# Issuing the output-row moves from SP instead of ACT in a DeltaNet and mixture-of-experts kernel

## The chip, the cores and the metric

One core of a Trainium2 chip runs the whole program. The metric is the device time in microseconds (us) of one execution; the median of three runs is quoted. One further execution is recorded by the hardware profiler. The engines are PE (TensorE, matrix products), ACT (ScalarE), DVE (VectorE), POOL (GpSimd) and SP (SyncE, which here only waits and issues DMAs). Each engine takes its own instructions strictly in order. ACT and SP both can issue DMAs; each has a queue of its own, q10 and q1 in the profile.

## The reference

The input is x of shape (2, 2048, 256). The first layer is a gated delta rule with 8 heads of 128 and three Householder steps per token, the second a mixture of 8 experts of which each token uses 2. Cut to what matters here:

```python
q = _short_conv(x @ Wq, conv_q)            # 4 taps over time, then silu
k = _short_conv(x @ Wk, conv_k)            # 3 keys per token
v = _short_conv(x @ Wv, conv_v)            # 3 values per token
def step(S, inp):                          # one token, state S is 128 x 128 per head
    S = S * jnp.exp(gt)[..., None, None]
    for i in range(nh):
        kS = jnp.einsum('bhd,bhde->bhe', ki, S)
        S = S + bi[..., None, None] * (ki[..., None] * (vi - kS)[:, :, None, :])
    o = jnp.einsum('bhd,bhde->bhe', qt, S)
o = o * jax.lax.rsqrt(jnp.mean(o * o, -1, keepdims=True) + 1e-05) * rms_weight
o = o * jax.nn.silu(x @ Wg)
x = _layernorm(x + o @ Wo)
x = _layernorm(x + experts(x))             # top 2 of 8, F = 816
```

## The kernel before

A setup stage splits x and the weights into pairs of 16-bit parts and stores them to HBM. Then comes the main loop, from about 100 to 4000 us, and last the router and the experts. The change touches only the main loop.

**Blocks.** The work of the loop is cut in 128 blocks: 16 (batch, head) pairs, each with 8 stretches of 256 tokens. The order is all 16 pairs of a stretch `tb`, then the next stretch. A block of 256 tokens has 8 chunks `c` (or `u`) of 32 tokens. For each chunk the three delta steps and the query make a 128-row triangular system, which is inverted in levels (`level_x`, `level_t`, `level_tt` on PE, copied out by `mask_x` on DVE and `keep_t`, `keep_tt` on ACT). Then the chunks run one after another through the state: `from_state`, `solve`, `update` on PE, with `keep_w(c)` on ACT writing the solution to `w_sol`. Rows 96 to 127 of `w_sol` hold the outputs of the 32 tokens.

**Bodies.** The engines are software pipelined. One body, written out by hand for each engine as a fixed list, works on five blocks at once: `k0` is the newest, `k1` to `k4` the ones one to four bodies older. Semaphores (class `Count`) connect the lists. For block `k3` the body of ACT ends the chunks with `keep_w(7, k3)`, then moves the output rows, and some operations later squares them:

- `move_outputs(k3)` (L1015 to L1021) waits for `keep_w(7)` and for the free buffer (`scaled`), and issues four DMAs, each of 32 partitions by two chunks, from `w_sol` to `o_rows` (64 rows of 512 B). This changes the partitions on which the rows lie, from 32 to all 128.
- `square_outputs(k3)` (L1024 to L1029) waits until all four have landed (`moved`), then computes the sums of squares.

After `square_outputs` ACT has `keep_t(6, 0)` and `keep_tt(6, 0)`, for which PE waits in `residual(0)` (L785, matmuls L792 and L793). Before `residual(0)` PE has `project(4)` (L692). Two operations behind `move_outputs` ACT has `keep_tt(4, 0)` (L1002), for which PE waits in `level_t(5, 0)` (L768, L780).

**SP.** For each (tb, head), that is for each body, SP does in this order:

- `body`: the small table `t_cur`;
- `load_next`: it waits until the last projection and the last convolution tap (`tapped`) of the block before are done, and loads the inputs of the next block: `x_cur` (L577, 259 KB), `w_cur` (L580, 1024 KB), `c_cur` (L581), `g_cur` (L582);
- `outputs`: it clears 128 rows of the experts' input (L600, 256 KB), waits for `y_buf` of the block five bodies back and stores it (L606, 128 KB);
- `pieces`: for the heads 0 to 13 it loads a piece of the experts' weights (L629, 224 KB, heads 0 to 11) and stores one that POOL has split (L639, 224 KB, heads 2 to 13), behind a wait for POOL's `e_low` (L1367).

`w_cur` and `x_cur` have two buffers each, so a load issued at the start of a body is needed about one body later.

Of the kernel before, what the change touches and what calls it, by code (L numbers as in the profile page):

```python
# [32 lines left out]
B, T, D = 2, 2048, 256  # L33
KT = D // P
H, NH, DH = 8, 3, 128
TAPS = 4
CH = 32
UN = 8
TB = CH * UN
NTB = T // TB  # L40
NIT = B * H * NTB
# [78 lines left out]
def at_least(eng, sem, value):  # L120

    if isinstance(value, int) and value <= 0:
        return
    eng.wait_ge(sem, value)


def build(nc, x_t, x_rows, w_all, w_z, conv_w, a_log, dt_bias, rms_w, w_o, consts, masks,
# [8 lines left out]
    with ctx:  # L136
# [244 lines left out]
        with ExitStack() as loop_scope:  # L381
            scope = loop_scope

            def ring(name, size, shape, dt):
# [52 lines left out]
            moved = [sem("moved0"), sem("moved1")]  # L437
            e_in = [sem("piece_in0"), sem("piece_in1")]
            e_out = [sem("piece_out0"), sem("piece_out1")]
            (sp_waited, act_waited, cleared, x_waited, pool_waited, e_high, e_low, zeroed) = map(sem, (  # L440
                "sp_waited", "act_waited", "cleared", "x_waited", "pool_waited", "piece_high", "piece_low", "zeroed"))
            squared, q_squared, g_made, scaled = map(sem, ("squared", "q_squared", "g_made", "scaled"))
            gate_done, ln_made, norm_made, o_squared, var_ln_made, rstd_made = map(sem, (
                "gate_done", "ln_made", "norm_made", "o_squared", "var_ln_made", "rstd_made"))
# [126 lines left out]
            with nc.Block() as block:  # L571
                @block.sync
                def _(sp):
                    def load(tb, head, res):

                        b, h = head // H, head % H
                        sp.dma_start(x_cur[res][:, :, :, 0:PW].rearrange("p a b c -> p (a b) c"),  # L577
                                     x_dram.rearrange("p (a c) -> p a c", a=2 * KT)[:, :, bass.ds(b * XW + tb * TB, PW)])\
                            .then_inc(loaded[res], 16)
                        sp.dma_start(w_cur[res][:].rearrange("p a b c -> p (a b c)"), w_dram[h]).then_inc(loaded[res], 16)  # L580
                        sp.dma_start(c_cur[res][:], conv_sb[:, h]).then_inc(loaded[res], 16)  # L581
                        sp.dma_start(g_cur[res][:], g_parts[:].rearrange("p n a -> p (n a)")[:, bass.ds((head * NTB + tb) * UN, UN)])\  # L582
                            .then_inc(loaded[res], 16)

                    clear_rows = x_slots.rearrange("(a b) d -> a (b d)", b=2)

                    def body(tb, head, new=True):

                        n = B * H * tb + head
                        if new:  # L590
                            done(sp, stated, 7, n - 8)
                            sp.sem_inc(sp_waited, 1)
                            sp.dma_start(t_cur[head % 8][:].rearrange("p a b -> p (a b)"),
                                         tables[:].rearrange("p n a b -> p (n a b)")[:, bass.ds((head * NTB + tb) * (4 * UN), 4 * UN)])\
                                .then_inc(tabled[head % 4], 16)

                    def outputs(tb, head, new=True):
                        n = B * H * tb + head
                        if new:
                            sp.dma_start(clear_rows[bass.ds(n * P, P), :], no_rows[:]).then_inc(cleared, 16)  # L600
                        d = n - STORED
                        if not isinstance(n, int) or 0 <= d < NIT:
                            done(sp, rows_kept, "outputs", d)
                            sp.sem_inc(sp_waited, 1)
                            dst = y_dram[d] if isinstance(d, int) else y_dram.rearrange("n p t -> (n p) t")[bass.ds(d * P, P), :]
                            sp.dma_start(dst, y_buf[(head - STORED) % 2][:]).then_inc(stored[(head - STORED) % 2], 16)  # L606

                    def load_next(tb, head):
                        n = B * H * tb + head
                        done(sp, projected, 7, n - 1)  # L610
                        sp.sem_inc(sp_waited, 1)
                        done(sp, tapped, 6, n - 1)
                        sp.sem_inc(sp_waited, 1)
                        at_least(sp, g_made, n)
                        sp.sem_inc(sp_waited, 1)
                        if head + 1 < B * H:
                            load(tb, head + 1, (head + 1) % 2)
                        else:
                            load(tb + 1, 0, 0)

                    def load_piece(e, c):

                        buf, (k, q) = e_raw[c % 2], (c // 4, c % 4)
                        at_least(sp, e_low, 12 * e + c - 1)
                        sp.sem_inc(sp_waited, 1)
                        src = (up_w, gp_w, down_w)[k].rearrange("e p c -> (e p) c")
                        c0, cut = q * QUARTER, (FT - 1) * D
                        if c < 11:
                            sp.dma_start(buf[:], src[bass.ds(e * P, P), c0:c0 + QUARTER]).then_inc(e_in[c % 2], 16)  # L629
                            return  # L630
                        sp.dma_start(buf[:, 0:cut - c0], src[bass.ds(e * P, P), c0:cut]).then_inc(e_in[1], 16)
                        sp.dma_start(buf[0:64, cut - c0:], src[bass.ds(e * P, 64), cut:]).then_inc(e_in[1], 16)
                        sp.dma_start(buf[64:65, cut - c0:], down_b[bass.ds(e, 1), :]).then_inc(e_in[1], 16)
                        sp.dma_start(buf[65:P, cut - c0:], src[bass.ds(e * P + 65, P - 65), cut:]).then_inc(e_in[1], 16)

                    def store_piece(e, c):
                        sp.wait_ge(e_low, 12 * e + c + 1)
                        sp.sem_inc(sp_waited, 1)
                        sp.dma_start(e_dram[c // 4][bass.ds(e * P, P), :, (c % 4) * QUARTER:(c % 4 + 1) * QUARTER],  # L639
                                     e_pair[c % 2][:]).then_inc(e_out[c % 2], 16)  # L640

                    def pieces(e, head):

                        if head < 12:
                            load_piece(e, head)
                        if 2 <= head <= 13:
                            store_piece(e, head - 2)

                    load(0, 0, 0)
                    for head in range(B * H):  # L650
                        body(0, head)
                        load_next(0, head)
                        outputs(0, head)
                        pieces(0, head)
                    with sp.Fori(1, NTB - 1) as tb:
                        for head in range(B * H):
                            body(tb, head)
                            load_next(tb, head)
                            outputs(tb, head)
                            pieces(tb, head)  # L660
                    for head in range(B * H):
                        body((NTB - 1), head)
                        if head + 1 < B * H:
                            load_next((NTB - 1), head)
                        outputs((NTB - 1), head)
                        pieces((NTB - 1), head)
                    for i in range(max(STORED, 4)):
                        outputs(NTB, i, new=False)
                    for i in range(2):
                        sp.wait_ge(e_out[i], 16 * (NPIECE // 2))  # L670
                        sp.wait_ge(stored[i], 16 * (NIT // 2))
                    sp.wait_ge(cleared, 16 * NIT)
# [260 lines left out]
                def _(act):  # L933
# [78 lines left out]
                        a(w_sol[k.i % 2][:, c], chain(k), ACT.Copy).then_inc(sol_kept.sem, 1)  # L1012

                    @at_stage
                    def move_outputs(k):  # L1015

                        done(act, sol_kept, 7, k.n)
                        at_least(act, scaled, k.n - 1)
                        act.sem_inc(act_waited, 1)
                        for c in range(4):  # L1020
                            act.dma_start(o_rows[k.i % 2][c * CH:(c + 1) * CH], w_sol[k.i % 2][96:128, c::4, :]).then_inc(moved[k.i % 2], 16)  # L1021

                    @at_stage
                    def square_outputs(k):  # L1024
                        act.wait_ge(moved[k.i % 2], 64 * (k.turn(2) + 1))
                        done(act, rows_kept, "queries", k.n - 1)
                        for i in range(2):
                            last = a(o_sq[:, i], o_rows[k.i % 2][:, i], ACT.Square, accum_out=o_sum[:, i:i + 1])
                        last.then_inc(o_squared, 1)  # L1029
# [12 lines left out]
                    def body(k0, k1, k2, k3, k4):  # L1042
# [12 lines left out]
                        keep_w(7, k3)  # L1055
                        silu(1, k0)
                        keep_t(4, 0, k1)
                        move_outputs(k3)
                        keep_tt(4, 0, k1)
                        first_tap(3, k0)  # L1060
                        keep_t(3, 1, k1)
# [986 lines left out]
```

## Time and profile before

| | |
|---|---|
| median of three runs | 4994.92 us (4980.66 to 4997.5) |
| profiled execution | 4980.66 us, its span 4978.8 us |
| busy in the span | PE 4230.5 us (85%), DVE 3658.3 (73%), ACT 3285.0 (66%), POOL 1648.1 (33%) |
| mean granted TensorE clock | 0.927 of 2.4 GHz |
| DMA, whole span | 490.64 MB, mean 99 GB/s |

The span reaches from the first to the last instruction. Busy time leaves out waiting and the issuing of DMAs. A row of the timeline says when an instruction started, how long it took, on which engine and line it is, what it writes and reads, and in brackets how long the engine had been idle before it and what ended that idle time. "issue" there means that the engine waited for nothing that the profile shows but its own sequencer. A "q" behind an engine's name is its sequencer, which issues DMAs. A DMA's row shows the issuing alone; the landing of the data is a separate number. 1.00 in a clock column is 2.4 GHz, 0.50 is 1.2 GHz.

### The profile page before, as it was taken

How to read it: one execution, taken by the hardware profiler on the slowest of the kernel's cores; microseconds unless marked ns; L12 is line 12 of the kernel's file. 1: busy time of each engine (PE TensorE's matmuls, PEld its weight loads, DVE VectorE, ACT ScalarE, POOL GpSimd, SP SyncE). 2: the span in 40 equal slices, each digit the busy share in tenths (PEclk: the TensorE clock that was granted, in tenths of full speed). 3: DMA queues.
4: the chain of work that ended last, by engine and by line, in shares of the span. 5: the costliest groups of instructions: out<-in, count | busy, mean ns of one | idle time of the engine just before them, and what ended most of it. 6: DMA issues, size and time to landing. Idle time of an engine off the chain costs nothing. (4 is left out here: it accounts for less than half of the span.)

```text
span 4978.8 us, 148669 instructions
## 1 busy us (share of the span) xinstructions
PE 4230.5 (85%) x47876; PEld 3759.0 (75%) x47876; DVE 3658.3 (73%) x10194; ACT 3285.0 (66%) x9028; POOL 1648.1 (33%) x1615
## 2 busy tenths in 40 slices
PE   2889988989898888898888898889889867599992
PEld 1788878888887777788788787888878745488882
DVE  6888888888888778788888788888888722344446
ACT  3777777777777677777777777777777611255552
POOL 3434333334433333343334343333434202200004
PEclk6999999999999999999999999999999877699996
DMA  6232223222223333222222222322222133366664
GB/s 234 69 95 73 66 77 86 79 70 77 77 71 70 76 77 70 70 77 79 82 75 77 77 67 77 92 76 67 75 77 75 43 88 108 123 236 227 230 236 140
DMA packets 363269, 490.64 MB, mean 99 GB/s; under 512 B 94080, under 2 KB 308096, under 8 KB 343680
## 3 DMA queue, kind: packets, MB, share of 16 engines
q1 hardware_dynamic: 304784, 437.06, 29.8%
q10 hardware_dynamic: 51568, 27.04, 1.9%
q0 software_dynamic: 6144, 16.79, 1.1%
q8 instruction: 419, 6.86, 0.6%
q14 instruction: 354, 2.90, 0.2%
HBM read 352.02 MB, written 107.75 MB: 92 GB/s over the span
## 5 line engine op out<-in xcount | busy, mean ns | idle before, releaser
L1134 DVE SCALAR_TENSOR_TENSOR conv_acc<-bank,c_cur,conv_acc 128x256 f32<-128x256 f32 x2688 | 1265.9, 477 | 274.3 <-ACT conv_acc L944 261.2
L692 PE MATMUL bank<-x_cur,w_cur 128*128 128x259 f16 (+1 forms) x6144 | 913.2, 288 | 29.4 <-DVE v_rows L1122 26.3
L1329 POOL TENSOR_TENSOR squares<-kq_t 128x768 f32<-128x768 f32 x128 | 187.7, 1467 | 1909.4 <-ACT kq_t L955 1909.4
L1195 DVE CAST_PREDICATED xs_lev<-mask,bank 128x256 f16<-128x256 uint16 x1536 | 662.2, 431 | 198.1 <-PE bank L756 174.4
L1002 ACT ACTIVATE invt<-bank 128x256 f16<-128x256 f32 x1280 | 509.7, 398 | 400.3 <-issue 374.5
L993 ACT ACTIVATE inv<-bank 128x256 f16<-128x256 f32 x1536 | 607.0, 395 | 167.8 <-PE bank L768 158.1
L692 PEld LDWEIGHTS bank<-x_cur,w_cur 128*128 128x128 f16 (+1 forms) x6144 | 577.7, 102 | 124.7 <-DVE v_rows L1122 27.2
L780 PE MATMUL bank<-invt,xs_lev 128*128 128x64 f16 x5120 | 379.9, 199 | 309.4 <-ACT invt L1002 305.2
L780 PEld LDWEIGHTS bank<-invt,xs_lev 128*128 128x128 f16 x5120 | 293.2, 101 | 341.5 <-ACT invt L1002 254.2
L944 ACT ACTIVATE conv_acc<-bank,c_cur 128x256 f32<-128x256 f32 x896 | 425.3, 475 | 156.5 <-PE bank L692 149.4
L824 PE MATMUL bank<-w_sol,k_rows 128*128 128x128 f32 x2048 | 474.6, 315 | 4.5 <-ACT w_sol L1012 4.1
L756 PE MATMUL bank<-inv,n_high 128*128 128x64 f16 x6144 | 450.8, 197 | 13.0 <-issue 2.7
L819 PE MATMUL bank<-rhs,inv_t 128*128 128x128 f32 x2048 | 447.4, 306 | 2.0 <-DVE rhs L1209 1.6
L813 PE MATMUL bank<-state,kq_t 128*128 128x128 f32 x2048 | 434.6, 304 | 8.5 <-DVE state L1216 7.7
L1342 POOL TENSOR_TENSOR n_t<-n_t,cst 128x512 f32<-128x512 f32 x256 | 326.1, 1274 | 329.5 <-DVE n_t L1162 329.5
L768 PE MATMUL bank<-xs_lev,invt 128*128 128x64 f16 x5120 | 377.1, 198 | 23.5 <-DVE xs_lev L1195 11.2
L756 PEld LDWEIGHTS bank<-inv,n_high 128*128 128x128 f16 x6144 | 321.2, 101 | 97.2 <-issue 43.5
L1209 DVE SCALAR_TENSOR_TENSOR rhs<-bank,t_cur,v_rows 128x128 f32<-128x128 f32 x1024 | 345.0, 337 | 30.8 <-PE bank L813 30.6
L1012 ACT ACTIVATE w_sol<-bank 128x128 f32<-128x128 f32 x1024 | 284.1, 278 | 118.4 <-PE bank L819 118.4
L1216 DVE SCALAR_TENSOR_TENSOR state<-state,t_cur,bank 128x128 f32<-128x128 f32 x1024 | 347.1, 339 | 11.5 <-PE bank L824 11.3
L1320 POOL TENSOR_TENSOR decay<-decay_tok,cst 128x512 f32<-128x512 f32 x256 | 320.7, 1274 | 99.5 <-ACT decay_tok L967 81.6
L768 PEld LDWEIGHTS bank<-xs_lev,invt 128*128 128x128 f16 x5120 | 292.4, 103 | 64.6 <-issue 26.7
(241 smaller groups left out, 10672.6 us busy)
## 6 DMA issues: line engine op xcount, KB each, us to landing
w_cur<-w_parts_scratch SPq DMA_DIRECT2D x128, 1024.0 KB, 7.1
ew<-e_parts_scratch SPq DMA_DIRECT2D x117, 896.0 KB, 6.2
x_cur<-x_parts_scratch SPq DMA_DIRECT2D x128, 259.0 KB, 7.0
x_slots<-no_rows SPq DMA_DIRECT2D x128, 256.0 KB, 7.1
e_parts_scratch<-e_pair SPq DMA_DIRECT2D x96, 224.0 KB, 6.0
o_rows<-w_sol ACTq DMA_DIRECT2D x512, 32.0 KB, 4.6
y_scratch<-y_buf SPq DMA_DIRECT2D x128, 128.0 KB, 6.3
y_in<-y_scratch SPq DMA_DIRECT2D x32, 512.0 KB, 4.1
```

What stands on the lines that cost most here:

```text
L692: last = mm(bank[i % 2][:, 0:PW], w_cur[k.i % 2][:, wp, kt, c * P:(c + 1) * P].bitcast(BF16 if wp else F16), x_cur[k.i % 2][:, xp, kt, 0:P ...
L756: last = mm(packed(LEVX[:, u * HP:(u + 1) * HP], l), n_high[k.i % 2][g][:, u], half(inv[k.i % R_LEV][g][:, u], l, 0), start=True, stop=True)
L768: last = mm(packed(LEVT[:, u * HP:(u + 1) * HP], l), by[:, u], half(xs_lev[g][l - 1][:, u], l, 0), start=True, stop=True)
L780: last = mm(packed(LEVTT[:, u * HP:(u + 1) * HP], l), xs_lev[g][l - 1][:, u], half(invt[k.i % R_LEV][g][:, u], l, 1), start=True, stop=True)
L813: mm(chain(k), kq_t[k.i % R_KQ][:, c].rearrange("p a b -> p (a b)"), state[:, k.i % (B * H)], start=True, stop=True).then_inc(ks_made.sem, 1)
L819: mm(chain(k), inv_t[k.i % R_INV][:, c], rhs[k.i % 2][:], start=True, stop=True).then_inc(sol_made.sem, 1)
L824: mm(chain(k), k_rows[k.i % R_ROWS][:, c], w_sol[k.i % 2][:, c], start=True, stop=True).then_inc(upd_made.sem, 1)
L944: a(conv_acc[(k.n + i) % 2][:], bank[i % 2][:, 0:TB], ACT.Copy, scale=c_cur[k.i % 2][:, c, 0:1])\
L993: a(half(inv[k.i % R_LEV][g][:], l, 0), packed(halves(LEVT), l), ACT.Copy).then_inc(t_kept.sem, 1)
L1002: a(half(dst, l, 1), packed(halves(LEVTT), l), ACT.Copy).then_inc(tt_kept.sem, 1)
L1134: v.scalar_tensor_tensor(acc, bank[at % 2][:, i:i + TB], c_cur[k.i % 2][:, c, i:i + 1], acc, ALU.mult, ALU.add).then_inc(tap_step.sem if i ...
L1195: v.copy_predicated(half(xs_lev[g][l - 1][:], l, 0), half(mask4[:, l], l, 0).bitcast(U16), packed(halves(LEVX), l)).then_inc(x_kept.sem, 1)
```

## The change

The four moves of a block are issued by SP and no longer by ACT. `move_outputs` is now a function of SP. It first waits that `o_rows` is free and then, ahead of each of the four DMAs, for the chunk `keep_w(4 + c)` of which the DMA takes the rows, where ACT had waited once for `keep_w(7)`. It stands at the end of SP's list, behind `load_next`, for the block three bodies older. In the same list the clear and the store of `y_buf` go from `outputs` into `body`, ahead of `load_next`, and `pieces` goes ahead of `load_next` too. After the last loads, SP's five closing turns call `body` (without the table and the clear) and `move_outputs`. ACT's list is unchanged but for the missing call.

```diff
-                    def outputs(tb, head, new=True):
-                        n = B * H * tb + head
                         if new:
                             sp.dma_start(clear_rows[bass.ds(n * P, P), :], no_rows[:]).then_inc(cleared, 16)
                         d = n - STORED
...
                             sp.dma_start(dst, y_buf[(head - STORED) % 2][:]).then_inc(stored[(head - STORED) % 2], 16)
+
+                    def move_outputs(n, i):
+
+                        if not isinstance(n, int) or 0 <= n < NIT:
+                            at_least(sp, scaled, n - 1)
+                            sp.sem_inc(sp_waited, 1)
+                            for c in range(4):
+                                done(sp, sol_kept, 4 + c, n)
+                                sp.sem_inc(sp_waited, 1)
+                                sp.dma_start(o_rows[i % 2][c * CH:(c + 1) * CH], w_sol[i % 2][96:128, c::4, :]).then_inc(moved[i % 2], 16)
...
                     with sp.Fori(1, NTB - 1) as tb:
                         for head in range(B * H):
                             body(tb, head)
+                            pieces(tb, head)
                             load_next(tb, head)
-                            outputs(tb, head)
-                            pieces(tb, head)
+                            move_outputs(B * H * tb + head - 3, head - 3)
...
                     for i in range(max(STORED, 4)):
-                        outputs(NTB, i, new=False)
+                        body(NTB, i, new=False)
+                        move_outputs(NIT + i - 3, i - 3)
...
                     @at_stage
-                    def move_outputs(k):
-
-                        done(act, sol_kept, 7, k.n)
-                        at_least(act, scaled, k.n - 1)
-                        act.sem_inc(act_waited, 1)
-                        for c in range(4):
-                            act.dma_start(o_rows[k.i % 2][c * CH:(c + 1) * CH], w_sol[k.i % 2][96:128, c::4, :]).then_inc(moved[k.i % 2], 16)
...
                         keep_t(4, 0, k1)
-                        move_outputs(k3)
                         keep_tt(4, 0, k1)
```

The order of the first and of the last stretch of 16 heads is changed in the same way as that of the loop.

## Rows read from the trace of the kernel before

**Rows 1.** Waits, whole run: who waited for whom, us in total, times, longest.
```profile
ACT invt L1002 <- issue: 374.5, 126, 4.6
PE bank L780 <- ACT invt L1002: 305.2, 126, 4.1
...
ACT o_sq L1028 <- DMA o_rows<-w_sol: 109.6, 88, 4.0
...
PE bank L792 <- ACT invt L1002: 55.2, 56, 2.9
```

**Rows 2.** Timeline of SP, one body: start us, us, what [idle before].
```profile
1130.54 0.62 SPq L577 DMA_DIRECT2D x_cur<-x_parts_scratch  x1
...
1132.49 3.30 SPq L582 DMA_DIRECT2D g_cur<-g_parts  x1
1136.01 0.53 SPq L600 DMA_DIRECT2D x_slots<-no_rows  x1
1136.91 0.34 SPq L606 DMA_DIRECT2D y_scratch<-y_buf  x1
...
1138.20 0.62 SPq L639 DMA_DIRECT2D e_parts_scratch<-e_pair  x1
...
1159.53 0.61 SPq L577 DMA_DIRECT2D x_cur<-x_parts_scratch  x1
```

**Rows 3.** Timeline of ACT, the same body.
```profile
1134.46 0.28 ACT L1012 ACTIVATE w_sol<-bank 128x128 f32<-128x128 f32 x1
...
1135.50 1.97 ACTq L1021 DMA_DIRECT2D o_rows<-w_sol  x3
1137.58 0.38 ACT L1002 ACTIVATE invt<-bank 128x256 f16<-128x256 f32 x1 [2.27 <-issue]
...
1142.62 0.31 ACT L1028 ACTIVATE o_sq<-o_rows 128x128 f32<-128x128 f32 x1 [1.58 <-DMA o_rows<-w_sol]
```

**Rows 4.** Timeline of PE, the same body.
```profile
1138.02 0.29 PE L780 MATMUL bank<-invt,xs_lev 128*128 128x64 f16 x4 [1.75 <-ACT invt L1002]
...
1141.77 0.84 PE L692 MATMUL bank<-x_cur,w_cur 128*128 128x259 f16 x6
1143.90 0.23 PE L792 MATMUL bank<-inv,n_high 128*128 128x128 f16 x1 [1.30 <-ACT invt L1002]
```

**Rows 5.** SP and ACT in two other bodies; windows view (clock third from last).
```profile
3080.53 0.62 SPq L577 DMA_DIRECT2D x_cur<-x_parts_scratch  x1
...
3091.03 0.31 ACT L1028 ACTIVATE o_sq<-o_rows 128x128 f32<-128x128 f32 x1
...
3108.11 0.61 SPq L577 DMA_DIRECT2D x_cur<-x_parts_scratch  x1
...
636.26 0.31 ACT L1028 ACTIVATE o_sq<-o_rows 128x128 f32<-128x128 f32 x1 [3.17 <-DMA o_rows<-w_sol]
...
655.95 0.62 SPq L577 DMA_DIRECT2D x_cur<-x_parts_scratch  x1
...
639.00:646.00 7.00, 7.00 (x43) 6.85 (x43) 3.92 (x14) 3.09 (x9) 4.02 (x4) 0.51 0.01 2
```

**Rows 6.** L577 (durations, first and last start), its first full body, and L1021's landings.
```profile
L577 SPq DMA_DIRECT2D x_cur<-x_parts_scratch x128: 577/602/669, 100.9 to 3889.3; - x128
...
186.56 0.58 SPq L577 DMA_DIRECT2D x_cur<-x_parts_scratch  x1
...
DMA to landing us min/median/max: 1.9/4.6/7.4
```

**Rows 7.** DMA view, 1139 to 1141 us, all queues.
```profile
DMA packets 681, 0.68 MB, mean 342 GB/s; under 512 B 209, under 2 KB 605, under 8 KB 660
```

**Rows 8.** The same, 1141 to 1143 us, by queue: packets, MB, share of 16 engines.
```profile
q1 hardware_dynamic: 310, 0.25, 36.9%
...
q10 hardware_dynamic: 40, 0.02, 2.8%
```

**Rows 9.** Timeline of POOL, the same body's piece.
```profile
1127.63 1.04 POOL L1367 TENSOR_TENSOR e_pair<-e_raw,e_pair 128x448 bf16<-128x448 f32 x1
```

More of the change, by code:

```diff
@@ L439, in build @@
             e_out = [sem("piece_out0"), sem("piece_out1")]
-            (sp_waited, act_waited, cleared, x_waited, pool_waited, e_high, e_low, zeroed) = map(sem, (
-                "sp_waited", "act_waited", "cleared", "x_waited", "pool_waited", "piece_high", "piece_low", "zeroed"))
+            (sp_waited, cleared, x_waited, pool_waited, e_high, e_low, zeroed) = map(sem, (
+                "sp_waited", "cleared", "x_waited", "pool_waited", "piece_high", "piece_low", "zeroed"))
             squared, q_squared, g_made, scaled = map(sem, ("squared", "q_squared", "g_made", "scaled"))
@@ L651, in _ @@
                         body(0, head)
+                        pieces(0, head)
                         load_next(0, head)
-                        outputs(0, head)
-                        pieces(0, head)
+                        move_outputs(B * H * 0 + head - 3, head - 3)
                     with sp.Fori(1, NTB - 1) as tb:
@@ L657, in _ @@
                             body(tb, head)
+                            pieces(tb, head)
                             load_next(tb, head)
-                            outputs(tb, head)
-                            pieces(tb, head)
+                            move_outputs(B * H * tb + head - 3, head - 3)
                     for head in range(B * H):
                         body((NTB - 1), head)
+                        pieces((NTB - 1), head)
                         if head + 1 < B * H:
                             load_next((NTB - 1), head)
-                        outputs((NTB - 1), head)
-                        pieces((NTB - 1), head)
+                        move_outputs(B * H * (NTB - 1) + head - 3, head - 3)
                     for i in range(max(STORED, 4)):
-                        outputs(NTB, i, new=False)
+                        body(NTB, i, new=False)
+                        move_outputs(NIT + i - 3, i - 3)
                     for i in range(2):
@@ L1014, in move_outputs @@
                     @at_stage
-                    def move_outputs(k):
-                        done(act, sol_kept, 7, k.n)
-                        at_least(act, scaled, k.n - 1)
-                        act.sem_inc(act_waited, 1)
-                        for c in range(4):
-                            act.dma_start(o_rows[k.i % 2][c * CH:(c + 1) * CH], w_sol[k.i % 2][96:128, c::4, :]).then_inc(moved[k.i % 2], 16)
-                    @at_stage
                     def square_outputs(k):
```

## The prediction

> **What bounds the kernel now.** I read four views in this order.
>
> First the whole run's waits [rows 1]. ACT, an engine that computes, stands idle for 374.5 us in 126 stalls "by issue" ahead of `keep_tt(4, 0)` (L1002). PE stands idle for 305.2 us in 126 stalls waiting for that same line. ACT then waits 109.6 us for the moved rows (L1028), and PE 55.2 us for what ACT does behind that wait. So the four `move_outputs` DMAs cost ACT, and through it PE, about 2.4 us in every body.
>
> That sum is not yet a gain, so second comes one body, engine by engine, with its zero at the start of SP's `x_cur` DMA, 1130.54 us [rows 2]. ACT ends the issue of the four moves at +6.93 us, and they have held it idle for 2.27 us [rows 3]. Its `square_outputs` starts at +12.08, held 1.58 us by the landing of the moves. PE idles 1.75 us at L780, finishes `project(4)` at about +12.07, idles another 1.30 us and starts `residual(0)` at +13.36 [rows 4]. The next `x_cur` is issued at +28.99 [rows 2].
>
> Third, the length of a body splits in two: D, from `x_cur` to the start of `square_outputs`, and R, from there to the next `x_cur`. Here D = 12.08 and R = 16.91. In the body at 3080.53, D = 10.50 and R = 17.08 [rows 5]. The same two rows, read for all 123 bodies from 186.56 to 3889.3 us [rows 6], give a mean D of 12.75 and a mean R of 17.36, with 89 bodies' R below 17.3. R hardly depends on D. A body lasts as long as its moved rows are late, plus a fixed rest. The mean body is (3889.3 - 186.56)/123 = 30.10 us.
>
> Fourth, what sets D. The last move is issued by +6.93 but its rows are used at +12.08, 5.15 us later, although the shortest landing in the run took 1.9 us [rows 6]. The DMA engines are full: between +8.5 and +10.5 us they move 342 GB/s [rows 7], and between +10.5 and +12.5 come the last 40 packets of ACT's queue (q10), beside 310 of SP's queue (q1) [rows 8]. The 1.28 MB of `x_cur` and `w_cur` stand in front of them.
>
> **The change, part by part.**
>
> *ACT loses the four issues.* That removes 2.27 us of idle in this body, 374.5/126 = 2.97 us on average [rows 1, 3]. PE's stall at L780 goes with it. If nothing else held, PE would reach the end of `project(4)` at 12.07 - 1.75 = +10.3 us, and ACT `square_outputs` at 12.08 - 1.58 - 2.27 = +8.2.
>
> *SP issues them instead, behind `load_next`.* SP ends `g_cur` at +5.25 [rows 2]. The neighbours of such an issue there take 0.34 to 0.62 us, and 0.22 us (no wait) to 0.37 us (a wait and an increment) lie between them. Four issues with five waits take 4 x 0.5 + 5 x 0.33 = 3.7 us, so the last ends near +8.9, against +6.93 before. `keep_w(7)` is done at +4.2 [rows 3] and holds nothing up. Queued behind the moves on SP are `t_cur`, the clear, the `y` store, the pieces and the next loads. None is due within 15 us, so that part costs nothing; if the cover were gone each would be 1 to 4 us late.
>
> *The landing, D'.* The lower bound is issue plus the shortest landing: 8.9 - 0.5 + 1.9 = +10.3. The moves are now in SP's own queue behind the loads, so they can't pass them; that queue is still at work after +10.5 [rows 8]. What helps: the clear, the `y` store, `e_raw` and `e_store` (256 + 128 + 224 + 224 KB) no longer compete with the moves from behind. What hurts: for 14 of 16 heads `e_raw` and `e_store` now go ahead of the loads. POOL ends the piece at 1128.67, 1.87 us before `x_cur` [rows 9]; two issues (0.36 + 0.62) and two waits fit in that, so `x_cur` is not issued later, but up to 448 KB lie in front of it. Upper bound: at the 342 GB/s of [rows 7], 1.3 us later than now, 12.75 + 1.3 = 14.0. I take 12.4, near today's 12.75, because it is backlog and not issue that sets it.
>
> The Trainium skill ("DMA: Bandwidth & Descriptors", section "Queues, rings and completion order") says that each DMA engine takes packets from its queues in turn, so that moves on ACT's queue would overtake part of the loads and lose that on SP's. The trace does not bear out much overtaking, since 40 q10 packets start more than 3 us after the last issue ended [rows 3, 8]; by the rule the sum would go by the upper bound, 14.0.
>
> *The rest, R'.* Its work is untouched. But the idle of PE is now in one piece: it ends `project(4)` at +10.3 and starts `residual(0)` 1.28 us after `square_outputs` (13.36 - 12.08), at 12.4 + 1.3 = +13.7. That is 3.4 us of idle in place of 1.75 and 1.30 apart. Of 46 bodies whose L780 stall [rows 4] is 2.7 us or more, 39 have TensorE's granted clock at its lower level (1.2 GHz) shortly after; of 75 with a shorter one, 38. Until now that low stretch fell mostly before `residual(0)`, in time that the moves cost anyway. It would now fall in R, where PE is nearly always busy. Price: after 3.17 us of waiting at 636.26 the clock is 0.51 for 7 us and R is 19.69, 2.8 more than 16.91, 0.4 us for each us at the low level [rows 5]. A usual low stretch lasts half as long: 1.4 us, times 39/46, 1.2 us. A part is in the mean of 17.36 already, so I add 1.1. Bounds: 0 and 2.8.
>
> *The edits to the order* (clear and `y` store in `body`, pieces ahead of `load_next`) have no price beyond D'. The five bodies after the last load have no loads in front of the moves: a gain of about 5 us at most in all.
>
> **Sum.** D' + R' = 12.4 + 17.36 + 1.1 = 30.86 us, 0.76 more than 30.10, times 123 = +93 us. The profiled execution took 4980.66 us (span 4978.8), the lowest of the three runs; the median is 4994.92. From the one 5074 comes out, from the other 5088. I say 5080 us.
>
> **Rivals.**
>
> *A: relief arrives.* If the moves land by about +9.5, ACT and PE are held no longer. The body falls to PE's own work: in the body at 3080.53 PE had no other wait and took 27.58 us [rows 5], and 1.75 of it is the stall of [rows 4], so some 26. That is -3.5 to -4 us, 123 times: 4500 to 4600 us. For it: 305.2 us of PE's waits point at the issue alone [rows 1]. Against it: the landing follows the load backlog, and SP issues later, not earlier. It decides on D' below 10.5. Chance 0.17.
>
> *B: the stall moves, the clock does not fall into R, or D' is near the lower bound.* With D' of 11.5 to 12.7 and R' of 17.36 a body takes 28.9 to 30.1 us: 4830 to 4990 us. For it: some bodies passed 2.9 us stalls at full clock. Against: 39 of 46. It ends on the other side or at no change. Chance 0.23.
>
> *C: the whole queue slips* behind the pieces. D' = 13.7 and R' = 18.5 give 32.2, +2.1 us, 5235 us. For it: the 448 KB. Against: they are issued 1.9 us before the loads, when the engines are idle. Chance 0.15. The page's rule named above would end here too.
>
> *The change does nothing*, since SP reaches the moves only when they are late: this is the forecast's own mechanism, and it would show as no change if the clock held. It is in B.
>
> **How the numbers follow.** Forecast 0.45 (its own range 4990 to 5170), A 0.17, B 0.23, C 0.15. The range leaves out A and the ends of B and C: 4860 to 5240. Within 0.3% (15 us) is what a measurement of this kernel can't tell from no change. Faster: A and two thirds of B, 0.32. Same: the rest of B and a little of the forecast, 0.10. Slower: 0.58.
>
> **What would show it.** "ACT invt L1002 <- issue" gone. The wait of ACT at L1028 up from 109.6 to some 450 us (3.5 us in each body), with D' about 12.4. PE's waits for L1002 at L780 nearly gone, those at L792 up from 55 to some 400 us. A low clock within 5 us after `residual(0)` in most bodies and R above 18. The prediction is wrong if `square_outputs` starts before +10.5 us (A), or if R stays at 17 (B).

## The result, and the profile after

The changed kernel takes 5211.15 us (median of four executions, 5154.57 to 5220.62) against 4988.82 us (four, 4980.66 to 4997.5; the 4994.92 us quoted for the kernel before are the median of three of these). The measured ratio, which is not that of the two medians, is 1.0422, with a 95% interval of 1.0344 to 1.0500: slower by 4.2%. The medians lie 222 us apart. The forecast was 5080 us, slower by 1.7%. The sign and the chain of waits came out as forecast, and the time lies in the wide range (4860 to 5240) but outside the 4990 to 5170 that belonged to the forecast itself. The size came out at more than twice what was forecast.

The profiled execution of the changed kernel took 5212.94 us, its span 5211.1 us. The mean granted clock of TensorE fell from 0.927 to 0.883. PE is busy for 4387.1 us in place of 4230.5, though it computes the same.

The waits of the whole run, changed kernel (engine line waited for: us, times, longest):

```profile
ACT o_sq L1027 <- DMA o_rows<-w_sol: 447.7, 119, 7.6
DVE v_sum L1223 <- issue: 374.4, 118, 6.9
PE bank L800 <- ACT invt L1010: 361.5, 111, 7.2
...
ACT invt L1010 <- PE bank L788: 48.9, 134, 4.5
```

The first two rows of [rows 1] are gone: no stall "by issue" ahead of `keep_tt(4, 0)` (now L1010) and next to none of PE in `level_t`. In their place ACT's wait for the moved rows has gone from 109.6 to 447.7 us, and PE's wait in `residual(0)` (now L800) from 55.2 to 361.5. Together ACT waits about as long as before (374.5 + 109.6 = 484 against 448). The stall has moved.

The `x_cur` loads, and the landings of the moves, changed kernel (durations in ns; first and last start in us):

```profile
L577 SPq DMA_DIRECT2D x_cur<-x_parts_scratch x128: 582/639/714, 101.4 to 4125.3; - x128
...
L613 SPq DMA_DIRECT2D o_rows<-w_sol x512: 585/638/1616, 189.9 to 4223.0; - x171
...
DMA to landing us min/median/max: 1.8/3.7/6.3
```

The first full body starts at 185.98 us, so the mean body is (4125.3 - 185.98)/123 = 32.03 us, 1.93 more than 30.10. Times 123 that is 237 us, about the whole difference of the spans (5211.1 - 4978.8 = 232). The change costs nothing outside the main loop.

One body of the changed kernel, SP, then ACT, then PE (timeline; start, us, what, idle before):

```profile
1507.58 0.65 SPq L577 DMA_DIRECT2D x_cur<-x_parts_scratch  x1
...
1509.62 2.96 SPq L582 DMA_DIRECT2D g_cur<-g_parts  x1
1512.85 3.11 SPq L613 DMA_DIRECT2D o_rows<-w_sol  x4
...
1541.58 0.65 SPq L577 DMA_DIRECT2D x_cur<-x_parts_scratch  x1
...
1519.64 0.31 ACT L1027 ACTIVATE o_sq<-o_rows 128x128 f32<-128x128 f32 x1 [3.62 <-DMA o_rows<-w_sol]
...
1516.84 0.84 PE L700 MATMUL bank<-x_cur,w_cur 128*128 128x259 f16 x6
1520.93 0.29 PE L800 MATMUL bank<-inv,n_high 128*128 128x128 f16 x1 [3.25 <-ACT invt L1010]
```

SP ends the fourth move 8.38 us after `x_cur`; `square_outputs` starts at +12.06 (D), held 3.62 us. PE is through with `project(4)` at about +10.1 and stands 3.25 us ahead of `residual(0)`. All of that is as forecast. But from `square_outputs` to the next `x_cur` it takes 21.94 us (R). The windows view of that stretch shows why (PE busy and instructions, PEld, DVE, ACT, POOL, then the granted clock):

```profile
1521.00:1524.50 3.50, 3.50 (x26) 3.22 (x27) 2.08 (x6) 3.21 (x8) 2.58 (x2) 0.50 0.02 5
1524.50:1528.00 3.50, 3.50 (x22) 3.50 (x21) 1.64 (x5) 0.97 (x5) 2.48 (x2) 0.50 0.00 0
1528.00:1531.50 3.50, 3.50 (x22) 3.33 (x22) 1.98 (x9) 0.69 (x4) 0.56 (x1) 0.50 0.00 0
1531.50:1535.00 3.50, 3.50 (x30) 3.06 (x28) 2.17 (x8) 2.15 (x6) 0.71 (x1) 0.80 0.00 0
1535.00:1538.50 3.50, 3.50 (x46) 3.24 (x44) 3.41 (x12) 3.49 (x10) 2.62 (x3) 1.00 0.00 0
```

For over 10 us after the idle the clock stays at 1.2 GHz (0.50), and PE, busy throughout, gets 22 to 26 matmuls done in 3.5 us in place of 46. DVE is busy for 1.6 to 2.1 and ACT for 0.7 to 3.2 of each 3.5 us.

The same numbers for all 123 bodies, read from the timeline and the clock's records:

| mean per body, us | before | changed |
|---|---|---|
| body | 30.10 | 32.03 |
| D | 12.75 | 12.35 |
| of it, the last move's issue ends at | 7.80 | 8.34 |
| of it, the last move lands at | 12.57 | 12.28 |
| R | 17.36 | 19.68 |
| low clock, whole body | 2.80 | 7.10 |
| low clock in R, from 1.3 us behind the start of `square_outputs` (about where `residual(0)` starts) | 0.40 | 5.79 |
| bodies with none in R | 108 of 123 | 20 of 123 |

The 20 bodies of the changed kernel with no low clock in R have a mean R of 17.25 us, as before. In 35 bodies it is low for some 3.3 us and R is 18.72. In 50 it is low for more than 6.9 us, on average 10.5, and R is 21.52. That is 0.41 us for each us at the low level, (21.52 - 17.25)/10.5, the price that the prediction took from one body.

### The profile page after: what moved, and what is told of

Read it like the earlier page. It is cut to its first block and busy times, and to the rows that moved or that the text cites. A ratio compares the mean times of both kernels' runs of the same rounds, so it can differ in the third digit from the quotient of the medians.

```text
span 5211.1 us, 149412 instructions
## 1 busy us (share of the span) xinstructions
PE 4387.1 (84%) x47876; PEld 3922.9 (75%) x47876; DVE 3641.6 (70%) x10194; ACT 3283.0 (63%) x9028; POOL 1648.1 (32%) x1615
## 5 line engine op out<-in xcount | busy, mean ns | idle before, releaser
L700 PE MATMUL bank<-x_cur,w_cur 128*128 128x259 f16 (+1 forms) x6144 | 884.0, 281 | 39.9 <-DVE v_rows L1120 26.3
L700 PEld LDWEIGHTS bank<-x_cur,w_cur 128*128 128x128 f16 (+1 forms) x6144 | 564.7, 100 | 131.7 <-DVE v_rows L1120 27.2
L1010 ACT ACTIVATE invt<-bank 128x256 f16<-128x256 f32 x1280 | 511.2, 399 | 50.1 <-PE bank L788 48.9
L832 PE MATMUL bank<-w_sol,k_rows 128*128 128x128 f32 x2048 | 494.8, 326 | 3.0 <-ACT w_sol L1020 2.7
L800 PE MATMUL bank<-inv,n_high 128*128 128x128 f16 x1024 | 173.9, 249 | 361.5 <-ACT invt L1010 361.5
L827 PE MATMUL bank<-rhs,inv_t 128*128 128x128 f32 x2048 | 469.1, 318 | 2.5 <-DVE rhs L1207 1.8
L821 PE MATMUL bank<-state,kq_t 128*128 128x128 f32 x2048 | 461.9, 321 | 8.7 <-DVE state L1214 7.7
L800 PEld LDWEIGHTS bank<-inv,n_high 128*128 128x128 f16 x1024 | 112.6, 112 | 394.0 <-ACT invt L1010 300.4
L764 PEld LDWEIGHTS bank<-inv,n_high 128*128 128x128 f16 x6144 | 306.5, 98 | 120.5 <-issue 74.2
L788 PE MATMUL bank<-invt,xs_lev 128*128 128x64 f16 x5120 | 368.0, 194 | 27.1 <-issue 27.0
L1027 ACT ACTIVATE o_sq<-o_rows 128x128 f32<-128x128 f32 x256 | 76.9, 301 | 447.7 <-DMA o_rows<-w_sol 447.7
```

Source lines behind the costliest of these rows:

```text
L700: last = mm(bank[i % 2][:, 0:PW], w_cur[k.i % 2][:, wp, kt, c * P:(c + 1) * P].bitcast(BF16 if wp else F16), x_cur[k.i % 2][:, xp, kt, 0:P ...
L764: last = mm(packed(LEVX[:, u * HP:(u + 1) * HP], l), n_high[k.i % 2][g][:, u], half(inv[k.i % R_LEV][g][:, u], l, 0), start=True, stop=True)
L788: last = mm(packed(LEVTT[:, u * HP:(u + 1) * HP], l), xs_lev[g][l - 1][:, u], half(invt[k.i % R_LEV][g][:, u], l, 1), start=True, stop=True)
L821: mm(chain(k), kq_t[k.i % R_KQ][:, c].rearrange("p a b -> p (a b)"), state[:, k.i % (B * H)], start=True, stop=True).then_inc(ks_made.sem, 1)
L827: mm(chain(k), inv_t[k.i % R_INV][:, c], rhs[k.i % 2][:], start=True, stop=True).then_inc(sol_made.sem, 1)
L832: mm(chain(k), k_rows[k.i % R_ROWS][:, c], w_sol[k.i % 2][:, c], start=True, stop=True).then_inc(upd_made.sem, 1)
```

## The experiments

Times are medians; ratios are to the kernel before, run on the same chip. "Body", D and R are means of 123 bodies of the profiled execution, and the low clock in R is counted as in the table above.

### e3, e4: the two halves of the change

The change moves the issue and reorders SP's list. e3 does the first alone (the moves on SP behind `load_next`, and behind them `outputs` and `pieces` as before), e4 the second alone (ACT keeps the moves):

```diff
# e3, against the changed kernel
                         body(tb, head)
-                        pieces(tb, head)
                         load_next(tb, head)
                         move_outputs(B * H * tb + head - 3, head - 3)
+                        outputs(tb, head)
+                        pieces(tb, head)
```

```diff
# e4, against the changed kernel
                         load_next(tb, head)
-                        move_outputs(B * H * tb + head - 3, head - 3)
...
                         keep_t(4, 0, k1)
+                        move_outputs(k3)
                         keep_tt(4, 0, k1)
```

> The moves are issued by SP directly behind load_next as in the changed kernel, but the clear, the store of y and the pieces stay behind them, in the order of the kernel before. Theory L: the order part matters little, 5150 to 5260 us, D 12.3 to 13. Rival C of the prediction (the pieces in front of the loads make the whole queue slip): this undoes it, D falls to about 11.5 and the time to 5000 to 5080. Rival S (SP's order): most of the loss gone.

> The order of SP's list as in the changed kernel (clear, store and pieces ahead of load_next), but ACT issues the moves as in the kernel before. Theory L: within 1% of the kernel before, a little faster if anything (the clear no longer competes with the moves), 4930 to 5000 us; the 374.5 us of issue stalls on ACT stay, D 12.3 to 12.8. Rival C: slower by 2% or more, since the pieces delay the loads and with them the moves.

e3: 5157.04 us, ratio 1.0327 (1.0295 to 1.0360); body 31.55, D 12.26, R 19.29, 5.4 us of low clock in R. e4: 4982.25 us, ratio 0.9978 (0.9951 to 1.0005); body 30.03, D 12.55, R 17.47. Its waits are those of the kernel before (last row: the moved rows, `square_outputs`):

```profile
ACT invt L996 <- issue: 364.4, 126, 5.0
...
PE bank L774 <- ACT invt L996: 294.1, 126, 4.5
...
ACT o_sq L1022 <- DMA o_rows<-w_sol: 111.0, 89, 4.0
```

So the issue by SP behind the loads makes most of the loss. The reordering alone is no change, as the prediction had it; with the moves on SP the median goes from 5157 to 5211 us with it, but the two intervals still touch, so that this part is left open.

The landing is nearly independent of who issues. In e4 the last issue ends at +7.61 and the rows land at +12.39. In the changed kernel, three quarters of a us later on another queue, they land at +12.28. The Trainium skill ("DMA: Bandwidth & Descriptors", section "Issuing engines are not separate DMA queues") says that DMAs run on the same 16 DMA engines whichever engine starts them. These two landings agree with it, 0.11 us apart.

What the moves stand behind is not the bulk of the loads alone. In the mean of the changed kernel's bodies `w_cur` (1024 KB) has landed at +8.10 us, `c_cur` (14 KB) at +9.36, `g_cur` (2 KB) at +11.54 and the last move at +12.28. In the body shown above, SP's queue keeps the DMA engines only 45.6% busy from 8.4 to 10.4 us after `x_cur` (1516 to 1518, DMA view):

```profile
DMA packets 455, 0.27 MB, mean 133 GB/s; under 512 B 292, under 2 KB 434, under 8 KB 434
```

In the kernel before it was 342 GB/s in nearly the same stretch of a body [rows 7]. So in these 2 us it is not full DMA engines that hold the moves of the changed kernel, and yet they land at about the same time. How much of D is due to the two small loads is not shown: no run leaves them out alone.

### e1: the moves ahead of the loads

```diff
                         pieces(tb, head)
-                        load_next(tb, head)
                         move_outputs(B * H * tb + head - 3, head - 3)
+                        load_next(tb, head)
```

> The changed kernel, with the four moves ahead of load_next in SP's list and not behind it. Nothing else differs. Theory L (the moves land late because the 1.28 MB of loads stand in front of them, and what they lose comes back as one idle stretch of PE in which the clock falls): the moves then wait for keep_w(7) alone, some 4 us into the body, and land 2 to 3 us after the last issue, that is about when ACT arrives. The wait of ACT at square_outputs falls from 447.7 us to below 100, PE's at residual(0) from 361.5 to below 60, the clock stays up, and a body takes 26 to 28 us in place of 32.0: 4400 to 4650 us, well below both kernels. Rival S (SP is too slow an issuer, or its new list is at fault): SP's list has the same instructions, so the time stays near 5200. Rival Q (on SP's queue the moves lose the turn that they had on ACT's): they still share the queue with the clear and the store, and only a part comes back: 4950 to 5100.

4466.65 us, ratio 0.8944 (0.8914 to 0.8974), granted clock 0.954. It is the fastest kernel of all, 10.6% below the one before and 14% below the changed one. Its first full body starts at 192.49 us; its `x_cur` loads and the landings of its moves:

```profile
L577 SPq DMA_DIRECT2D x_cur<-x_parts_scratch x128: 583/642/1591, 101.7 to 3403.4; - x128
...
L613 SPq DMA_DIRECT2D o_rows<-w_sol x512: 585/633/1917, 186.9 to 3490.2; - x171
...
  ACT o_sq L1027: 3.9, 2
...
DMA to landing us min/median/max: 1.8/2.0/6.2
```

The body is (3403.4 - 192.49)/123 = 26.11 us. The median landing falls from 3.7 to 2.0 us, ACT's wait for the rows from 447.7 to 3.9 us in the whole run (third row), and PE's idle from 3.59 to 0.27 us in each body. The moves are the same four DMAs by the same engine; only what stands in front of them differs. One body, SP:

```profile
1403.26 5.12 SPq L613 DMA_DIRECT2D o_rows<-w_sol  x4
1408.88 0.66 SPq L577 DMA_DIRECT2D x_cur<-x_parts_scratch  x1
```

The loads still come once per body, and no wait of the main loop for `x_cur` or `w_cur` shows in the list.

The gain over the changed kernel has two parts. PE's idle is 3.32 us per body shorter, and the clock is low for 0.42 us of a body in place of 7.10, which at 0.41 us for each is worth 2.7 us. Together that is 6.1 us, against 5.92 (32.03 - 26.11) measured.

### e7: how much of that is ACT's issuing

The kernel before, ACT still issuing, but the loads held back until the rows of the block in flight are squared:

```diff
                         n = B * H * tb + head
+                        at_least(sp, o_squared, n - 2)
+                        sp.sem_inc(sp_waited, 1)
```

> The kernel before, the moves still issued by ACT, but load_next waits also until square_outputs of the block whose rows are being moved has been made, so that no load stands ahead of the moves or beside them. Against the version with the moves on SP ahead of the loads (4467 us, 26.1 us per body) this prices the issuing by ACT alone. If ACT's four issues cost PE what the chain of waits says (305 to 375 us in all, 2.5 to 3 us in each body), the body takes 28.5 to 29 us and the kernel 4760 to 4830 us, and the wait at square_outputs is nearly gone. If the issues cost nothing once the landing is early (PE catches up behind them), it is about 4470 to 4550 us. If instead the later loads come too late for the next body, it is above 4993 us, with PE or ACT waiting for x_cur or w_cur.

4755.21 us, ratio 0.9559 (0.9518 to 0.9600); body 28.30, both just below what was expected if the issues cost what the waits say. The wait for the moved rows is down to 7.9 us in the whole run, and the issue remains:

```profile
ACT invt L1004 <- issue: 305.7, 126, 3.5
PE bank L782 <- ACT invt L1004: 238.1, 126, 3.1
```

So, from before (30.10) by way of e7 (28.30) to e1 (26.11), the loads in front of the moves cost 1.80 us per body and ACT's issuing 2.19. e7 and e1 also differ in the order of SP's list, which e4 showed to be worth nothing in the kernel before, and in when the loads start. But PE's idle per body, 2.05 us in e7 and 0.27 in e1, accounts for most of the 2.19. The issuing is what the change set out from in [rows 1]: it is real, 269 us in 123 bodies, but the changed kernel, which took it away first, got nothing for it.

### e6: half the weights

The changed kernel, with the low parts of `w_cur` loaded once at the start and never again, 512 of 1024 KB per body (every head is computed with the low parts of head 0, so e6 does not compute the same).

```diff
-                        sp.dma_start(w_cur[res][:].rearrange("p a b c -> p (a b c)"), w_dram[h]).then_inc(loaded[res], 16)
+                        sp.dma_start(w_cur[res][:, 0].rearrange("p b c -> p (b c)"), w_dram[h][:, 0:KT * HC]).then_inc(loaded[res], 16)
```

> The changed kernel, but w_cur is reloaded in each body with its high parts alone, 512 KB in place of 1024; the low parts are those of head 0 throughout, so the reload of the low parts is left out. Theory (the moves lie behind the backlog of the loads in SP's queue): 512 KB less at some 340 GB/s land 1.5 us earlier, D falls from 12.35 to about 10.9, the wait at square_outputs from 3.6 to about 2.1 us, R from 19.7 to about 18.5 as less of it runs at the low clock: 29.4 us per body, 4850 to 4950 us. Rival (SP's own issuing, the last of which ends at 8.3 us, and the moves' own time of flight set D): D stays within 0.3 us of 12.35 and the time within 1% of 5211.

4633.4 us, ratio 0.9325 (0.9290 to 0.9360); body 27.55, D 9.75, R 17.80, ACT's wait for the rows 154.3 us in the run. The last move is issued at +7.67 and lands at +9.61. The direction is that of the backlog, and the rival (SP's issuing sets D) falls. The size was missed, in D (2.6 us less, not 1.5) and in the time (4633 us, not 4850 to 4950). The 2.6 us are not all transfer time of 512 KB: `w_cur` itself landed 1.97 us earlier (6.13 against 8.10), which is 266 GB/s and not the 340 that I had divided by. `g_cur` behind it landed 3.16 us earlier (8.38 against 11.54), and SP was through with issuing the moves 0.67 us earlier. From its last issue to the landing e6 takes 1.94 us, near the 1.8 of the shortest landing, so there SP's issuing does set D. With D below 10.5 the kernel is where the prediction had put its case A; the body of some 26 us of that case is not reached (27.55).

### e2, e8, e5: filling PE's idle

If the long idle is what sends the clock down, useless work on PE in that idle must make the changed kernel faster. The first matmul of `project(4)` is repeated (22 times in e2 and e5, 10 in e8; some 2.4 and 1.1 us of PE), into the bank that the real one then overwrites:

```diff
+                        for _ in range(22 if c == 4 else 0):
+                            mm(bank[i % 2][:, 0:PW], w_cur[k.i % 2][:, 0, 0, c * P:(c + 1) * P].bitcast(F16),
+                               x_cur[k.i % 2][:, 0, 0, 0:PW].bitcast(F16), start=True, stop=True)
```

e2 and e8 are the changed kernel with them, e5 is the kernel before with them.

> The changed kernel, with the first matmul of project(4) repeated 22 times ahead of the real ones, 259 columns each, 2.4 us of PE work at the high clock inside the 3.6 us that PE idles before residual(0). The output is the same. Theory L, by its clock part: the moves land at the same time (D 12.4), but the clock no longer falls, so R goes from 19.7 back to about 17.1 and a body takes 29.5 us: 4880 to 4950 us, although more work is done. If the clock is not what makes R longer (rival: ACT and DVE, which have slipped behind PE, need the time), R stays at 19.7 and the time stays at 5200 or rises by what of the added work does not fit.

> The changed kernel with the first matmul of project(4) repeated 10 times (about 1.1 us of PE work in each body, in the idle ahead of residual(0)), between the changed kernel with none (5211 us, 5.8 us of low clock in R) and with 22 (5029 us, 1.3 us of it). If the clock in R is what costs, by how long PE has idled before it, the time lies between the two, 5080 to 5150 us, and the mean R of those bodies that have no low clock in it stays at 17.3 whatever the count. Rival: the time lost in R comes with the late rows themselves: then R with no low clock in it would already be above 18.

> The kernel before, with the first matmul of project(4) repeated 22 times (the same repeats that took the changed kernel from 5211 to 5029 us). They compute nothing that is used. In the kernel before PE idles only about 0.45 us (PE's waits for the line behind residual(0), 55.2 us over 123 bodies) to 1.3 us ahead of residual(0), and 108 of its 123 bodies have no low clock in R. If the repeats help only by keeping TensorE from the one long idle stretch, they must cost here: 2.4 us of PE work less the idle that they fill, +1.0 to +1.9 us in each body, 5110 to 5230 us. Rival: the repeats help whatever the issue of the moves (by an order or a timing that they shift): then this one is faster too, below 4950 us.

| | us | ratio (interval) | body | D | R | low clock in R | PE's wait in residual(0), whole run |
|---|---|---|---|---|---|---|---|
| changed | 5211.15 | 1.0422 (1.0344 to 1.0500) | 32.03 | 12.35 | 19.68 | 5.79 | 361.5 |
| e8, 10 repeats | 5083.35 | 1.0237 (1.0186 to 1.0287) | 31.23 | 12.48 | 18.75 | 3.18 | 201.8 |
| e2, 22 repeats | 5029.35 | 1.0072 (1.0051 to 1.0093) | 30.69 | 12.49 | 18.20 | 1.26 | 106.6 |
| e5, before with 22 | 5172.86 | 1.0419 (1.0376 to 1.0462) | 31.78 | 12.79 | 18.99 | 0.28 | |

More work makes the changed kernel 3.5% faster (5029 against 5211 us), with D and ACT's wait where they were (463.5 us in e2). The rows are still late in e2:

```profile
ACT o_sq L1030 <- DMA o_rows<-w_sol: 463.5, 121, 8.0
...
PE bank L803 <- ACT invt L1013: 106.6, 78, 4.4
```

The same repeats make the kernel before 4.2% slower, where they have no long idle to fill. That rules out that they help by themselves. e8 lies between, inside the expected 5080 to 5150. R of the bodies without low clock is 17.06 in e8 and 17.4 in e2, so late rows alone, without a low clock behind them, do not lengthen R. e2 did not come back all the way, and its 5029 us miss the expected 4880 to 4950: 94 of its bodies run R at full clock, but the other 29 do not, and their mean R is 20.9. Where the idle would have been short the repeats themselves should take time, as they do in e5; in e2 this part was not measured by itself.

### e9: the idle in one piece without SP

Is it SP's new list, or only the place of the idle? e9 is the kernel before, with ACT's call moved down:

```diff
                         keep_t(4, 0, k1)
-                        move_outputs(k3)
                         keep_tt(4, 0, k1)
...
+                        move_outputs(k3)
                         square_outputs(k3)
```

> The kernel before (ACT issues, SP's order as it was), with ACT's move_outputs called directly ahead of square_outputs in place of ahead of keep_tt(4, 0). So PE's stall at level_t(5, 0) is gone and all of its idle comes in one piece ahead of residual(0), as in the changed kernel, though SP's list is untouched. Theory (a low stretch that begins at residual(0) lasts about twice as long as one that begins at level_t: with 2.7 to 3.3 us of idle ahead 7.5 us against 4.0): R rises to 19.5 or more with 6 us or more of low clock in it, D to about 13.5 to 14 as the issue ends near +11 us; 33 to 34.5 us per body, 5340 to 5520 us. Rival (the long low stretches come from SP's new list or from the moves on its queue): R stays at 17.4 to 18.5 with low stretches of 3.4 us as in the kernel before, 31 to 32.5 us per body, below 5290 us.

5501.1 us, ratio 1.1063 (1.1017 to 1.1110); body 34.17, D 13.99, R 20.18, 7.6 us of low clock in R, all as the theory had it. In one body PE idles 3.09 us and the clock then is at the low level for some 10 us (timeline, then windows):

```profile
512.30 0.22 PE L792 MATMUL bank<-inv,n_high 128*128 128x128 f16 x1 [3.09 <-ACT invt L1002]
```

```profile
513.00:516.50 3.50, 3.50 (x26) 3.24 (x23) 2.42 (x5) 2.69 (x6) 2.81 (x3) 0.50 0.02 5
516.50:520.00 3.50, 3.50 (x19) 3.50 (x20) 1.09 (x6) 0.69 (x3) 1.77 (x2) 0.50 0.00 0
520.00:523.50 3.50, 3.50 (x24) 3.04 (x23) 2.20 (x7) 0.92 (x4) 1.27 (x1) 0.55 0.00 0
523.50:527.00 3.50, 3.50 (x42) 3.40 (x41) 2.88 (x10) 3.37 (x7) 0.58 (x1) 1.00 0.00 0
```

Over all bodies: in the kernel before 46 idles of 2.7 us or more end at `level_t(5, 0)`. A low stretch goes with 39 of them; 35 of these last 3.4 us and one 10.2. At `residual(0)` the changed kernel has 72 such idles, each with a low stretch, of which 45 last 10.2 or 13.7 us; e9 has 108, of which 68 are followed by 10.2 us or more.

But these idles are also longer, 4.1 us in the mean in the changed kernel and 4.5 in e9 against 3.1 at `level_t`. Among idles between 2.7 and 3.5 us alone, 1 of 42 at `level_t` goes with 10 us or more, against 13 of 26 (changed) and 12 of 23 (e9) at `residual(0)`. So the place counts at equal length too. The length counts beside it: in the 38 bodies of the changed kernel and the 79 of e9 in which the clock had fallen more than 1 us before PE started again, no low stretch was shorter than 6.8 us, and at `level_t` in the kernel before it never fell that early. That e9 is slower than the changed kernel goes with its longer idles and its later landing (D 13.99), not with the place alone.

### e10: squaring later

The changed kernel, with `square_outputs(k3)` four operations later on ACT, so that `residual(0)` no longer stands behind the late rows, and DVE's `sum_squares(k3)` (L1223) three operations later, ahead of `keep_v(0, k1)`:

```diff
-                        square_outputs(k3)
                         keep_t(6, 0, k1)
                         keep_tt(6, 0, k1)
                         silu(3, k0)
                         keep_w(4, k2)
+                        square_outputs(k3)
```

> The changed kernel with square_outputs four operations later in ACT's list (behind keep_t(6, 0), keep_tt(6, 0), silu(3) and keep_w(4)) and DVE's sum_squares of it three later, ahead of keep_v(0). The moved rows land as late as before, but PE's residual(0) no longer waits behind them. Theory (the lateness costs only through what is queued behind the wait on ACT): PE's idle of 3.6 us in each body goes, no low clock in R, 27.5 to 29 us per body, 4650 to 4850 us; what is left of ACT's wait is 1 to 2.5 us in each body. Rival: the wait only moves; PE and DVE then wait for keep_w(4), first_tap(4) or v_sum, and the time stays above 5050 us.

5140.88 us, ratio 1.0308 (1.0259 to 1.0358), body 31.67, so the rival was right. ACT's wait for the rows falls to 264.0 us, but PE now stands a few operations further on:

```profile
PE bank L739 <- DVE v_sum L1223: 280.1, 116, 6.2
ACT o_sq L1027 <- DMA o_rows<-w_sol: 264.0, 109, 5.9
```

PE needs there what DVE does behind `sum_squares`. PE still idles 2.97 us per body, and 6.3 us of R are at the low clock. The late rows are squared on ACT, their sums are needed on DVE and the rows again on POOL, and to defer the first two by a few operations was not enough.

## Why the prediction came out as it did

*What bounds the kernel* held in its first half: D is the landing of the moved rows behind the loads; e1, e4, e6 and e7 show it from four sides. Not shown is that full DMA engines make it late: in the changed kernel these move 133 GB/s from +8.4 to +10.4 in place of 342, and D' is nearly the same. That R is a "fixed rest" did not hold.

*ACT loses the issues, PE's first stall goes*: right ([rows 1] against the waits after).

*SP's issue*: forecast to end at +8.9, measured +8.34 (3.11 us for four in the body shown, where 3.7 were reckoned). It does not set D.

*D'*: 12.4 forecast, 12.35 measured. The bounds were 10.3 and 14.0. Case A, relief, did not come. What it would have given is shown by e1: its price, a body of some 26 us, is e1's 26.11, and its 4500 to 4600 us for the kernel stand against 4466.65.

*R' is the step that failed.* "A usual low stretch lasts half as long: 1.4 us, times 39/46, 1.2 us. A part is in the mean of 17.36 already, so I add 1.1." Measured: 19.68 - 17.36 = 2.32 us. Both other factors of the term held: the price is 0.41 us for each us at the low clock (forecast 0.4), and 103 of 123 bodies have some of it in R. The length was wrong. I carried the usual length of a low stretch, 3.4 us, from where it began in the kernel before, at `level_t`, to `residual(0)`, where it was to begin. There it lasts 10 us or more in 50 of 123 bodies; the mean over all is 5.79 us in R. 5.79 less the 0.40 that was there already, by 0.41, is 2.2 us: nearly all of the 2.32, where the prediction had 1.1. Part of it is the place and part the idle, which was longer than 3.5 us in 46 bodies; the runs do not divide the two. The rows to see it with were there: in the example in which ACT had waited 3.17 us, PE had stood 2.86 us ahead of L792, and the clock was 0.51 for 7 us [rows 5]. The kernel before has just one other idle of 2.7 us or more at that line, and with it goes a low stretch of 10.2 us. I used the example for the price and then halved its length to the "usual" one, which came from the other place. That row times 39/46 would have given 2.4 us.

*The sum.* D' + R' = 12.35 + 19.68 = 32.03 against 30.86 forecast: 1.17 us in 123 bodies, 144 us, against a miss of 131 (5211 - 5080) by the medians.

*Rivals.* C had nearly the right time (5235 us) by luck: its D' of 13.7 did not come, and its R' of 18.5 was 1.2 too low. The rule of the Trainium skill ("DMA: Bandwidth & Descriptors", section "Queues, rings and completion order"), by which D' would have been 14.0 because the moves lose their turn on ACT's queue, does not show in it: D' was 12.35. B fell with R.

*The signs named beforehand*: ACT's wait at `square_outputs` 447.7 us (some 450), PE's in `residual(0)` 361.5 (some 400), the first row of [rows 1] gone, R above 18.

**What stays open.** Why a low stretch that begins at `residual(0)` goes on for so much longer than one at `level_t`. e9 shows that it does not hang on SP's list or the queue; the idle's length explains a part of it, and the rest goes with the place in the body. What PE does in the first us after each differs, but no run varies that alone. Open too is why the moves land 4 us after `w_cur`, though the DMA engines are less than half busy for two of these.

## What to carry to other kernels

A small DMA that something waits for belongs ahead of bulk loads that nothing waits for yet; which engine issues it comes second. Here the order is worth more (5211 to 4467 us by two swapped calls), and the issuing paid only once the order was right. An issue taken off a computing engine was no gain while the data that it moves was late. When a stall moves, price it where it lands: look for the few bodies that already have it there, and take all of what they show, the clock after it too.

## What the runs showed of the hardware that was not expected

The low stretch of TensorE's clock around an idle of PE of 2.7 to 3.5 us lasted 10 us or more in 1 of 42 cases at one place of the loop and in 13 of 26 at another some 6 us further on, though PE was counted busy behind both. In this kernel each us of it cost 0.41 us in R, and 2.4 us of useless matmuls in the idle bought back 182 us of 5211. A load of 2 KB (`g_cur`), issued by +4.75 us behind 1.28 MB of others, landed at +11.54, 3.4 us after the 1024 KB in front of it, and the moves behind it at +12.28. Halving the 1024 KB let the moves land 2.67 us earlier (12.28 to 9.61).
